# A perceiver block on one core: in the first cross attention's lead-in each chunk of latents is normalised and turned ahead of the early step

## The reference

```python
x = x + L0_xattn(ctx_1024, layernorm(x), mask, g1, b1, g2, b2, Wq, Wkv, Wout)   # changed: its lead-in
x = x + L0_attn(layernorm(x), ...)      # a gated linear recurrence
x = x + L0_ffn(layernorm(x), ...)
x = x + L1_xattn(layernorm(x), ctx_1024, ctx_1024, mask, ...)
x = x + L1_attn(layernorm(x), ...)
x = x + L1_ffn(layernorm(x), ...)       # 16 experts
```

```python
xn = layer_norm(x, g1, b1)              # x is the context here
ln_lat = layer_norm(latents, g2, b2)    # latents is layernorm(x): two norms in a row
q = ln_lat @ Wq
kv = concat([xn, ln_lat], axis=1) @ Wkv # 257 + 32 keys for each batch
out = softmax(q k / 8, masked) v        # 16 heads of 64, then @ Wout
```

## Time and profile before

| | us |
|---|---|
| median of 3 runs (lowest, highest) | 1928.56 (1924.19, 1932.86) |
| time of the profiled execution | 1924.67 |
| span of the profiled execution, first to last instruction | 1922.8 |
| lead-in, from the first latent tile normalised to the first score | 39.31 to 67.53 |
| PE, DVE, ACT, POOL busy over the span | 88%, 82%, 78%, 44% |
| mean granted TensorE clock | 0.932 |

### The profile page before, as it was taken

One profiled execution on the slowest core, in us unless ns is written; L12 is line 12 of the kernel. 1 busy time (PEld: TensorE's weight loads), 2 busy tenths in 40 slices (PEclk: granted clock), 3 DMA queues, 4 the chain that ended last, 5 costly groups with the idle time before them and its releaser, 6 DMA issues. The chain is left out here.

```text
span 1922.8 us, 49940 instructions
## 1 busy us (share of the span) xinstructions
PE 1699.3 (88%) x13527; PEld 1340.6 (70%) x13527; DVE 1580.5 (82%) x5121; ACT 1505.9 (78%) x4166; POOL 837.3 (44%) x1318
## 2 busy tenths in 40 slices
PE   5799999999999999996540689999999899979998
PEld 4688888888888888873330656767666566667776
DVE  5888889888888888868779689999999678866665
ACT  4788888888888888866696599999999688855544
POOL 2644444444444444422220034444444277725555
PEclk6799999999999999998575899999999899969999
DMA  6466666666666666650000069999989610026665
GB/s 172 116 166 163 164 165 164 168 168 166 161 165 168 164 161 165 168 137 1 1 1 0 24 181 247 248 246 246 252 252 242 168 34 0 1 30 106 107 109 92
DMA packets 234174, 263.88 MB, mean 137 GB/s; under 512 B 26712, under 2 KB 188556, under 8 KB 233968
## 3 DMA queue, kind: packets, MB, share of 16 engines
q1 hardware_dynamic: 231776, 260.60, 55.1%
q10 hardware_dynamic: 2080, 1.97, 0.3%
q0 software_dynamic: 240, 0.37, 0.1%
HBM read 90.35 MB, written 4.74 MB: 49 GB/s over the span
## 5 line engine op out<-in xcount | busy, mean ns | idle before, releaser
L897 PE MATMUL a_out<-a_probT,a_xn 128*128 128x256 f32 x1024 | 264.4, 382 | 3.7 <-DMA a_probT<-a_blocks 2.1
L817 ACT ACTIVATE a_prob<-a_neg,a_nmax 128x289 f32<-128x289 f32 x512 | 266.5, 524 | 1.3 <-DVE a_nmax L716 1.0
L1864 ACT ACTIVATE b_prob<-b_neg,b_nmax 128x257 f32<-128x257 f32 x512 | 259.5, 512 | 5.2 <-DVE b_nmax L1799 4.8
L669 POOL TENSOR_TENSOR a_xn<-a_z,g 128x256 f32<-128x256 f32 x128 | 94.4, 738 | 379.8 <-DVE a_z L758 379.8
L887 PE MATMUL a_score<-a_xnT,a_qT 128*128 128x290 f32 x1536 | 241.9, 306 | 2.9 <-DVE a_qT L769 2.9
L887 PEld LDWEIGHTS a_score<-a_xnT,a_qT 128*128 128x128 f32 x1536 | 211.4, 190 | 44.4 <-issue 44.4
L716 DVE CUSTOM_DVE_ANT_0 a_neg<-a_score,a_bias 128x289 f32<-128x289 f32 x512 | 208.5, 456 | 39.0 <-PE a_score L887 34.7
L825 ACT ACTIVATE a_prob<-a_prob,a_rinv 128x289 f32<-128x289 f32 x512 | 232.5, 527 | 9.6 <-DVE a_rinv L774 6.8
L1799 DVE CUSTOM_DVE_ANT_0 b_neg<-b_score,b_bias 128x257 f32<-128x257 f32 x512 | 188.6, 420 | 24.1 <-PE b_score L1969 16.3
L897 PEld LDWEIGHTS a_out<-a_probT,a_xn 128*128 128x128 f32 x1024 | 176.3, 192 | 18.6 <-DMA a_probT<-a_blocks 3.7
L733 DVE STREAM_TRANSPOSE a_blocks<-a_prob 128x1024 f32<-128x1024 f32 x128 | 159.3, 1245 | 13.5 <-ACT a_prob L825 9.1
(11 more groups left out here) (469 smaller groups left out, 4431.9 us busy)
## 6 DMA issues: line engine op xcount, KB each, us to landing
a_probT<-a_blocks SPq DMA_DIRECT2D x512, 192.0 KB, 3.5
b_probT<-b_blocks SPq DMA_DIRECT2D x256, 256.0 KB, 4.6
a_raw<-in_ctx SPq DMA_DIRECT2D x128, 128.0 KB, 3.0
b_raw<-in_ctx SPq DMA_DIRECT2D x64, 256.0 KB, 4.3
m_wide<-expert_weights SPq DMA_DIRECT2D x128, 128.0 KB, 8.2
a_kept<-keep SPq DMA_DIRECT2D x32, 257.0 KB, 3.3
b_kept<-keep SPq DMA_DIRECT2D x32, 257.0 KB, 4.9
b_v_rows<-ctx_tail_values SPq DMA_DIRECT2D x32, 256.0 KB, 4.7
```

The source lines that it names most:

```text
L817: nc.scalar.activation(prob[:, par, grp, 0:KEYS0], neg[:, grp, :], ACT.Exp, bias=nmax[:, par, grp:grp + 1], scale=-1.0, accum_out=rsum[:, ...
L897: nc.tensor.matmul(out_ps[:, half, 0:2 * P], xn[:, j, kt, :], probT[:, u, :, kt, half * (P // 2):(half + 1) * (P // 2)], start=(kt == 0), ...
L1864: nc.scalar.activation(prob[:, (j + 5) % 4, grp, :], neg[:, par, grp, :], ACT.Exp, bias=nmax[:, par, grp:grp + 1], scale=-1.0, accum_out=r ...
```

## The change

Normalising and turning a chunk become functions, `norm_latents(c)` on DVE and `turn_latents(c)` on PE. Both are called for chunk 0 before the loop, and inside the loop for chunk `c + 1`: on DVE behind the multiplication of chunk `c` and ahead of the early step, on PE ahead of the early step. No instruction is added or removed, no semaphore's count changes, and ACT, POOL and SP run the same instructions in the same order.

```diff
@@ vector
-                for c in range(CHUNKS):
-                    u = c % 2
+                def norm_latents(c):
                     wait(dve, lat_turned, c - 1)
                     for j in range(2):
                         t = c * 4 + j
-                        last = nc.vector.tensor_scalar(z2[:, u, j, :], k.x[:, t * D:(t + 1) * D], mean[:, t:t + 1], twice[:, t:t + 1],
+                        last = nc.vector.tensor_scalar(z2[:, c % 2, j, :], k.x[:, t * D:(t + 1) * D], mean[:, t:t + 1], twice[:, t:t + 1],
                                                        ALU.subtract, ALU.mult)
                     last.then_inc(z2_ready, 1)
+
+                norm_latents(0)
+                for c in range(CHUNKS):
+                    u = c % 2
                     wait(dve, stored[u], c // 2 * 16)
                     dve.wait_ge(z2_ready, c + 1)
                     dve.wait_ge(z2_act, c + 1)
...
+                    if c + 1 < CHUNKS:
+                        norm_latents(c + 1)
                     if c in EARLY:
                         step(-1, EARLY[c])
@@ tensor
-                for c in range(CHUNKS):
+                def turn_latents(c):
                     pe.wait_ge(z2_ready, c + 1)
                     pe.wait_ge(z2_act, c + 1)
                     wait(pe, lat_copied, c - 1)
                     for j in range(4):
                         last = nc.tensor.transpose(bank[c % 2][:, j * P:(j + 1) * P], z2[:, c % 2, j, :], k.ident[:])
                     last.then_inc(lat_turned, 1)
+
+                turn_latents(0)
+                for c in range(CHUNKS):
+                    if c + 1 < CHUNKS:
+                        turn_latents(c + 1)
                     if c in EARLY:
                         pe.wait_ge(lat_copied, c)
                         step(-1, EARLY[c])
```

## The result

The changed kernel takes 1929.29 us (median of 12 runs) against 1924.41 of the kernel before (12 runs): a ratio of 1.0028, 95% interval 1.0015 to 1.0042, so 5.4 us slower by the ratio, between 2.9 and 8.1 (the medians differ by 4.9). A second series gave 1.0037, 1.0023 to 1.0052. The forecast was +3.9, with a range of 1925 to 1938 for the time.

What follows compares the result with a forecast made beforehand. The lead-in, hung on a DVE-PE-ACT loop, was taken to set the first score's date. Terms +2.19, +1.56, +1.29 and -1.16 made +3.9 us: 1928.6 against the profiled execution, 1932.5 against the median; range 1925 to 1938.

Steps and rivals of the forecast that it cites:

- the loop: Lead-in cycle of DVE normalising, PE turns and query, ACT high part, DVE low part; 6.99 us per two chunks before.
- early step 3: Third part of the lead-in: low part at 64.34 instead of 59.30, adding +1.29 us.
- Early step 1 and 2: First two parts of the lead-in: low parts at 48.60 and 57.15, adding +2.19 and +1.56 us.
- The new wait of the query: On PE, early step 1's query stands behind turns needing chunk 2 normalised: start 46.01 instead of 43.83, 2.18 late.
- the long pair: On DVE, two normalisations directly behind a multiplication meet POOL's add and take 1.54 us instead of 0.59.
- the round of 8.55: Lead-in from early step 1's low part to early step 2's: 8.55 us instead of 6.99.
- the upper bound: Lead-in with pairs of chunks 5, 6 and 7 all long: +5.7 us, +7 with multiplications stretched by POOL too.
- To the first score: Last part of the lead-in, chunk 6 already normalised and turned: gives back 1.16 us, first score at 71.4.
- Nothing downstream gives it back: Behind the first score, DVE (74 to 90 us) and PE (from 200 us) have no waits to shorten, so +3.9 stays.
- The rival of the absorbed delay: Clock rises before the first score, returning 1.4 us there and about 0.9 on queries; 1928.6 us, chance 0.18.
- The pair does fill DVE's wait: Rival: moved pairs fit in DVE's waits for ACT's high part, lead-in shortens by 2.3 us to 1926.2; chance 0.13.
- The longer low clock: Rival: TensorE stays at the lower clock two further steps behind the first score, +11.7 us, 1940; chance 0.04.

Runs made afterwards that it cites:

- the small add: POOL's add of b2 cut to one column in 128, in both kernels; to the first score 25.44 us in the changed kernel, 22.82 in the one before.
- DVE's part alone: Changed kernel with PE's loop left as in the kernel before, only DVE reordered; 24.32 us to the first score, ratio 0.9994 to before.

## Why the prediction was right

The time, the sign and the loop were right; the sum was too small by 2.8 us up to the first score, in early step 3 above all, and 2.0 came back behind it, which the sum had put at nothing.

- *Early step 1 and 2: right to 0.02 us.* Predicted from the multiplication of chunk 1: low parts at 5.70 and 14.25; measured 5.69 and 14.24. The new wait of the query, the long pair and the round of 8.55 are as worked out. That POOL's add makes the pairs long is shown by the small add, that the query's place makes them count by DVE's part alone, which has the same long pairs and no loss. The rule of the Trainium skill (SBUF — State Buffer, "Who interferes with whom") on the port pair that VectorE and GpSimd share holds in these runs: 0.60 beside an add of 0.24, 1.54 beside one of 1.30.
- *Early step 3: mis-sized, +1.29 predicted, +3.70 measured.* Its low part stands 23.84 behind the multiplication of chunk 1 instead of 16.40, +7.44, of which +3.74 were there at early step 2. The step that failed is "the pair of chunk 5, which had found POOL between small instructions: 0.59" and the one behind it, "0.09 to the multiplication of chunk 5 (59.05), 0.61 to the pair of chunk 6". The measured durations are 0.89 for the multiplication of chunk 4 instead of 0.69, 1.32 for the pair of chunk 5 beside L693, 1.77 for the multiplication of chunk 5, which reads two tiles in SBUF and ended 0.55 behind POOL's add, and 1.54 for the pair of chunk 6 instead of 1.13. Over the lengths in the sum these are 0.20, 0.73, 1.08 and 0.41 more, together the missing 2.4. The small add, which leaves 0.70 of the 1.77, shows POOL's add as its cause; for the 1.32 it is argued only from what stands beside it. I had let only the normalisations meet POOL; multiplications "stretched by POOL as well" stood in the upper bound alone.
- *To the first score: -1.16 predicted, -0.77 measured*; the pair of chunk 7 was long (1.54 for 1.13). The first score is 6.67 late instead of 3.9. The bounds of the sum went to +7, but only with stretched multiplications, for which the sum had no term.
- *"Nothing downstream gives it back": wrong by 2.0.* Over four profiles each, the multiplication of chunk 1 to the last projection takes 830.6 and 825.9: +4.7. The prediction's own sign for this, distances behind the first score that differ by over 1 us, came: 801.4 and 799.1 in the first pair. The rival of the absorbed delay had priced a higher clock at the first scores at 1.4 and 0.9; it was there in all four profiles of the changed kernel and in two of the kernel before, so it gives 0.7 of the mean, and loads and later stretches at the lower clock the rest. So it is luck in part that the forecast's +3.9 lies near the measured 4.7 of the stage: two errors of opposite sign, -2.8 and +2.0, met.
- *"No change under 0.5%, 9.6 us, can be told from none by measuring": wrong.* Twelve runs of each gave a ratio of 1.0028 with an interval of 1.0015 to 1.0042, which leaves 1 out.
- *The rivals.* The pair does fill DVE's wait when PE's order is left alone (2.02 to 0.55), but the lead-in then runs into the store of chunk 4, so that even this is worth 0.3 us only. The prediction had read the old lead-in as the loop alone and left out that its last part already waited 0.35 for this store. The longer low clock did not come: 1.00 was granted over the first ten us behind the first score.

## What to carry to other kernels

Work that is moved ahead of a wait on one engine fills the wait; the same work moved ahead of the instruction that others wait for lengthens the loop. Here DVE's half of the edit was free and the loss came with PE's, so each engine's reordering is worth trying by itself. Before moving a VectorE instruction beside one of GpSimd, add most of the length of GpSimd's instruction to its price: 0.95 us for a pair of normalisations beside an add of 1.30, and 1.08 for a multiplication with two SBUF inputs beside one of 1.26. And follow a gained date to the end of the stage: 1.4 us won at the first score were lost again behind two waits of 1.5 us for loads.

## What the runs showed of the hardware

A VectorE multiplication of two SBUF tiles, 0.69 us alone, took 1.77 beside a GpSimd add of 1.26 that had started 0.04 us ahead of it. Counted from the multiplication of chunk 1, the first score repeats to 0.03 us between profiles of one kernel, and the third low part of the kernel before to 0.15 (16.40 to 16.55), while the multiplication itself started between 38.8 and 43.7 us over all profiles. And TensorE's granted clock over the same ten us of one program was 0.78 in one execution and 1.00 in another; the twelve matmuls at its start took 3.24 and 1.85 us.
